# A macaron layer on one core: ScalarE rounds the steps' turns instead of VectorE, and the stages are ordered by new lengths

## The chip, the core and the metric

One core of a Trainium2 chip. The metric is the device time of one execution in microseconds, the median of several runs. TensorE is PE in the profile, VectorE DVE, ScalarE ACT, GpSimd POOL, SyncE SP (it only issues DMAs here); PEld is TensorE's loading of weights.

## What is computed

`x` has 4 batches of 512 rows of 512 numbers, all float32. Three sublayers, each added to `x`: half a mixture-of-experts FFN, an attention-like layer, half the FFN again.

```python
x = x + 0.5 * ffn(layernorm(x))
x = x + attn(layernorm(x))
x = x + 0.5 * ffn(layernorm(x))

def ffn(x):                                  # 8 experts, 2 per row
    gates = softmax over the two largest of x @ gate_w
    routed = sum over the two: gate * (gelu(x @ w1[e] + b1[e]) @ w2[e] + b2[e])
    return routed + gelu(x @ shared_w1 + shared_b1) @ shared_w2 + shared_b2

def attn(x):                                 # 32 heads x 8 channels x 8 frequencies
    z = causal_conv4(x @ W_mem); k_val, s_raw = z[..., :256], z[..., 256:]
    p_w = exp(clip(score_scale * s_raw, -20, 20) + log_w)
    phi = k_val[..., None] * theta
    num_re, num_im = cumsum(p_w * cos(phi)), cumsum(p_w * sin(phi))    # along the rows
    den = cumsum(p_w)
    out_re = sum over frequencies of (num_re * q_re + num_im * q_im) / den
    out_im = sum over frequencies of (num_im * q_re - num_re * q_im) / den
    y_val, y_gate = split(out_re @ W_re + out_im @ W_im)               # per head
    return (y_val * silu(y_gate)) @ W_out
```

## The kernel before

**The work.** The FFN runs as 8 jobs (`JOBS`: first FFN of batches 0 to 3, second FFN of batches 0 to 3). A job `q` loads rows (`fetch`), normalises them (`load`, `norm`), turns them (`turn`, 4 tiles of 128 rows), makes gate logits (`chunks`, `logits`, `rank`, `gates`, `gT`), and computes the shared expert (`hidden`, 4 matmul groups, and `acc`, 4). The jobs form 6 groups `g` (the last two have two jobs each). For each group the rows are sorted by expert into blocks of 128 (`place`, `scatter`, `slots`, `rows`), 15 blocks in a group of one job and 23 in one of two, 106 in all. A block is a chain over engines: GpSimd gathers its rows (`bring`), TensorE turns them (`x`, L907), ScalarE copies them to SBUF (`x`, L1081), TensorE multiplies (`one`, L916), ScalarE copies (`one`, L1089), TensorE turns (`mid`, L924), ScalarE applies gelu (`mid`, L1098), TensorE multiplies (`two`, L932), ScalarE scales (`two`, L1111), GpSimd adds the rows to DRAM (`add`, L1744).

The attention of a batch `b` has a head, 16 steps and a tail. Head: `a_load` to `a_turn`, `a_mem` (TensorE L951, and the convolution on VectorE, L1451 and L1454), `a_p`, `a_fall`, `a_den` (VectorE on 32 partitions), `a_q`, `a_spread`. Tail, per half of the heads: `c_out` (TensorE, then VectorE L1565, then a transfer into `outT`), `o_gate` (L985, silu on ScalarE, the product `o_mul` on VectorE), and at the end `o_rows` (L994).

**A step** `(b, n)` treats one half of the heads and one frequency on a 128 x 512 tile. It is what VectorE does most:
- `c_turn` on VectorE (`phases`): L1507 multiplies `k_val` by `theta`, in turns, and writes it as integers, which rounds it; L1509 multiplies again and subtracts the integers, which leaves the fraction of a turn. Both write into `trig[:, n % 2]`, so they wait until the sums of step n-2 have read it.
- `c_turn` on ScalarE (`waves`): absolute value (L1183), sine (L1185), cosine as a sine (L1186). The sine needs a table that gelu, silu and exp don't share; where the table changes a load stands in front.
- `c_scan` on VectorE: two running sums (L1520).
- `c_times`: two products with the queries `qx` (L1527, L1532), which SP loads per step (`c_query`).
- `c_sum`: two to four additions (L1543, L1545, L1551, L1553).

```python
VE.tensor_scalar(trig_int[:, s, 0, :], kept(b, half), th, None, ALU.mult).then_inc(*phase_int.of((b, n)))
vec.wait_ge(*phase_int.at((b, n)))
VE.scalar_tensor_tensor(trig[:, s, 1, :], kept(b, half), th, trig_int[:, s, 0, :],
                        ALU.mult, ALU.subtract).then_inc(*phase_made.of((b, n)))
```

**What sets the order.** Each engine is a queue in program order, and waits on semaphores at its head. The order of all stages is made when the program is built: `piece(engine, stage, length, *after)` names a stage's length in us and what it follows, `orders()` plays the queues with these lengths (an engine takes, of the stages that could start, the one with the longest way to the end), and each engine's loop issues its stages in that order. `HOP` is added to every handoff. Ways are corrected by tables of numbers, `PARTS`, `KINDS` and `URGENT`. The steps' stages on VectorE come behind everything else (`way[k] -= 10000.0`).

## Time and profile before

| | us |
|---|---|
| median of 3 runs | 1149.53 |
| lowest, highest | 1144.08, 1149.84 |
| the profiled execution | 1146.77 |
| its span | 1145.5 |
| TensorE busy | 1014.8 |
| VectorE busy | 728.5 |
| ScalarE busy | 642.0 |
| GpSimd busy | 486.2 |
| DMA, mean rate | 151 GB/s |

The span is the time from the first to the last instruction; the execution's own time is 1.3 us longer. A busy engine is one with an instruction under way. The page has the sums; where an engine waits, and for what, is in the views of waits, stretches and timelines.

### The profile page before, as it was taken

The page shows a single profiled execution, that of the slowest core. Times are in us where ns is not written, and L with a number is a line of the kernel's source. Part 1 is how long each engine was busy: PE and PEld are TensorE (multiplying, and loading weights), DVE is VectorE, ACT ScalarE, POOL GpSimd, SP SyncE. Part 2 cuts the span into 40 slices and gives each one's busy share as a digit, 9 for nine tenths or more (in the row PEclk, how much of TensorE's full clock was granted, in tenths as well). Part 3 has the DMA queues.
Part 4 walks back from the last instruction along what each step waited for, and adds up shares of the span by engine and source line. Part 5 has one row for each costly group of instructions (what it writes and reads, how often), then busy time and mean ns, then how long its engine had stood idle before and what let it go on. Part 6 is the DMA issues. An engine that isn't in the chain of part 4 may idle for free. (4 is left out here: it accounts for less than half of the span.)

```text
span 1145.5 us, 11321 instructions
## 1 busy us (share of the span) xinstructions
PE 1014.8 (89%) x3424; PEld 559.0 (49%) x3424; DVE 728.5 (64%) x1210; ACT 642.0 (56%) x1100; POOL 486.2 (42%) x449
## 2 busy tenths in 40 slices
PE   5989999779899898899999799978997999999992
PEld 3456544446345554344554445444554544446671
DVE  2310119879799988979998999899999721200000
ACT  4334334775674776655687666339778733224441
POOL 3444540556414334335334324714654412245642
PEclk9989999899999899999999899989999999999997
DMA  9966563793834776825587953347885735226666
GB/s 317 328 184 132 97 166 82 192 275 62 207 101 92 172 205 164 223 66 141 126 218 163 228 156 84 94 124 177 177 212 134 167 46 96 70 92 112 129 100 111
DMA packets 69201, 172.53 MB, mean 151 GB/s; under 512 B 12579, under 2 KB 12579, under 8 KB 67015
## 3 DMA queue, kind: packets, MB, share of 16 engines
q0 software_dynamic: 32576, 72.44, 34.8%
q1 hardware_dynamic: 35270, 89.74, 25.0%
q10 hardware_dynamic: 1296, 9.63, 2.4%
q8 instruction: 30, 0.49, 0.2%
q14 instruction: 29, 0.23, 0.1%
HBM read 112.86 MB, written 68.33 MB: 158 GB/s over the span
## 5 line engine op out<-in xcount | busy, mean ns | idle before, releaser
L932 PE MATMUL yps<-w_all,hidden_sb 128*128 x424 | 212.5, 626 | 15.7 <-ACT hidden_sb L1098 15.5
L916 PE MATMUL hps<-w_all,hidden_sb 128*128 x848 | 206.9, 389 | 11.0 <-ACT hidden_sb L1081 10.7
L1720 POOL DMA_INDIRECT xs<-x_normal,rows_i x106 | 121.8, 1149 | 198.9 <-PE xps L907 141.6
L916 PEld LDWEIGHTS hps<-w_all,hidden_sb 128*128 128x128 f32 x848 | 159.7, 195 | 49.4 <-issue 31.1
L1744 POOL DMA_INDIRECT x_rows<-ys,rows_i x56 | 105.2, 1878 | 147.6 <-ACT ys L1111 137.9
L1520 DVE TENSOR_TENSOR_SCAN run<-pwx,trig 128x512 f32<-128x512 f32 x128 | 149.4, 1209 | 20.8 <-ACT trig L1186 20.4
L1111 ACT ACTIVATE ys<-yps,slots 128x512 f32<-128x512 f32 x106 | 72.6, 686 | 110.8 <-PE yps L932 80.4
L932 PEld LDWEIGHTS yps<-w_all,hidden_sb 128*128 128x128 f32 x424 | 80.8, 200 | 87.9 <-issue 85.5
L874 PE MATMUL yps<-sw_sb,hidden_sb 128*128 128x512 f32 x256 | 120.1, 613 | 0.0
L862 PE MATMUL hps<-xnT,sw_sb 128*128 128x512 f32 x256 | 117.8, 612 | 2.1 <-issue 2.1
L1706 POOL DMA_INDIRECT slots<-told,dest_i x64 | 78.1, 1220 | 51.0 <-DVE cmp_a L1389 32.2
L994 PE MATMUL misc<-turns_sb,tail_sb 128*128 128x512 f32 x192 | 85.0, 592 | 0.0
L907 PE MATMUL xps<-ident,xs 128*128 128x128 f32 x424 | 66.8, 283 | 19.0 <-DMA xs<-x_normal,rows_i 6.4
L1527 DVE TENSOR_TENSOR trig<-run,qx 128x1024 f32<-128x1024 f32 x64 | 78.1, 1220 | 4.4 <-DMA qx<-q_cols 3.9
L862 PEld LDWEIGHTS hps<-xnT,sw_sb 128*128 128x128 f32 x256 | 48.9, 196 | 64.0 <-issue 63.5
L1532 DVE TENSOR_TENSOR qx<-run,qx 128x1024 f32<-128x1024 f32 x64 | 78.1, 1220 | 0.0
L1089 ACT COPY hidden_sb<-hps 128x256 f32<-128x256 f32 x106 | 39.4, 372 | 65.6 <-PE hps L916 60.6
L1744 POOL DMA_INDIRECT sum_rows<-ys,into_i x28 | 49.8, 1780 | 59.6 <-ACT ys L1111 56.9
L1081 ACT COPY hidden_sb<-xps 128x512 f32<-128x512 f32 x106 | 62.3, 590 | 21.3 <-PE xps L907 16.2
L874 PEld LDWEIGHTS yps<-sw_sb,hidden_sb 128*128 128x128 f32 x256 | 46.6, 192 | 54.8 <-issue 54.8
L907 PEld LDWEIGHTS xps<-ident,xs 128*128 128x128 f32 x424 | 52.2, 146 | 43.2 <-issue 24.6
L1183 ACT ACTIVATE trig<-trig 128x512 f32<-128x512 f32 x64 | 40.5, 632 | 54.8 <-DVE trig L1509 53.8
(201 smaller groups left out, 1541.8 us busy)
## 6 DMA issues: line engine op xcount, KB each, us to landing
qx<-q_cols SPq DMA_DIRECT2D x64, 512.0 KB
w_all<-in_w_experts SPq DMA_DIRECT2D x8, 1024.0 KB
x_normal<-xin SPq DMA_DIRECT2D x32, 256.0 KB
xin<-x_rows SPq DMA_DIRECT2D x32, 256.0 KB, 7.1
turns_sb<-in_w_out ACTq DMA_DIRECT2D x3, 1536.0 KB, 7.9
xin<-in_x SPq DMA_DIRECT2D x16, 256.0 KB, 6.0
sum_rows<-ys SPq DMA_DIRECT2D x16, 256.0 KB
xin<-sum_rows POOLq DMA_DIRECT2D x16, 256.0 KB, 5.9
```

The source lines that it names most:

```text
L862: t = PE.matmul(hps[:, bank, :], sw1_sb[:, c, n * P:(n + 1) * P], xnT[:, c, :], start=c == 0, stop=c == KC - 1)
L874: t = PE.matmul(yps[:, bank, :], hT[:, n, tb * P:(tb + 1) * P], sw2_sb[:, n, :], start=False, stop=n == SC - 1)
L907: t = PE.transpose(xps[:, bank, c * P:(c + 1) * P], xs[:, j % NX, c * P:(c + 1) * P], ident[:, :])
L916: t = PE.matmul(hps[:, bank, 0:H], xT[:, j % 2, c, :], w_all[:, bass.ds(expert[j] + c * H, H)], start=c == 0, stop=c == KC - 1)
L932: t = PE.matmul(yps[:, bank, :], hb[:, j % 2, ec, :], w_all[:, bass.ds(expert[j] + (KC * H + ec * D), D)], start=ec == 0, stop=ec == EC - 1)
L994: t = PE.matmul(misc[:, bank, :], yT[:, v, tb * P:(tb + 1) * P], wout_sb[:, v, :], start=v == 0, stop=v == VT - 1)
L1520: t = VE.tensor_tensor_scan(run[:, c, :], pwx[:, n // M, :], trig[:, n % 2, c, :], 0.0, ALU.mult, ALU.add)
L1527: VE.tensor_tensor(trig[:, n % 2, :, :], run[:, :, :], qx[:, n % NQX, :, :], ALU.mult).then_inc(*real_made.of((b, n)))
L1532: VE.tensor_tensor(qx[:, n % NQX, :, :], back, qx[:, n % NQX, :, :], ALU.mult).then_inc(*imag_made.of((b, n)))
L1706: GE.indirect_dma_start(slots_dram[g], bass.IndirectOffsetOnAxis(dest_i[:, g % 2, t, r:r + 1], 0), told[:, g % 2, first_tile + t, r, :], N ...
L1720: GE.indirect_dma_start(xs[:, j % NX, :], None, xn_rows[PAIR_OF[g]], bass.IndirectOffsetOnAxis(rows_i[:, g % 2, j:j + 1], 0)).then_inc(*xs ...
L1744: GE.indirect_dma_start(INTO[g][side], bass.IndirectOffsetOnAxis(at[:, g % 2, j:j + 1], 0), ys[:, j % 2, :], None, compute_op=ALU.add).the ...
```

## The change

ScalarE gets a stage `c_count` for each step: it multiplies `k_val` by `theta` and writes integers. VectorE's `c_turn` keeps only the multiplication and subtraction, and waits for ScalarE's count. ScalarE's wait for the sums of step n-2 stands in the new stage.

```diff
+            def count_turns(b, n):
+                half, m = divmod(n, M)
+                if b > 0 or n >= 2:
+                    last = (b, n - 2) if n >= 2 else (b - 1, STEPS + n - 2)
+                    act.wait_ge(*(out_summed if last[1] % M else added).at((*last, 0)))
+                if (b, n) == (0, 0):
+                    act.wait_ge(*weighing.at(21))
+                act.wait_ge(*convolved.at((b, half, CW - 1)))
+                SE.activation(trig_int[:, n % 2, 0, :], kept(b, half), ACT.Copy,
+                              scale=theta_sb[:, half, m:m + 1]).then_inc(*turns_counted.of((b, n)))
+
...
+                elif stage == "c_count":
+                    count_turns(*at)
...
             def phases(b, n):
                 half, m = divmod(n, M)
                 s = n % 2
-                th = theta_sb[:, half, m:m + 1]
-                if b > 0 or n >= 2:
-                    last = (b, n - 2) if n >= 2 else (b - 1, STEPS + n - 2)
-                    vec.wait_ge(*(out_summed if last[1] % M else added).at((*last, 0)))
-                vec.wait_ge(*convolved.at((b, half, CW - 1)))
-                VE.tensor_scalar(trig_int[:, s, 0, :], kept(b, half), th, None, ALU.mult).then_inc(*phase_int.of((b, n)))
-                vec.wait_ge(*phase_int.at((b, n)))
-                VE.scalar_tensor_tensor(trig[:, s, 1, :], kept(b, half), th, trig_int[:, s, 0, :],
+                vec.wait_ge(*turns_counted.at((b, n)))
+                VE.scalar_tensor_tensor(trig[:, s, 1, :], kept(b, half), theta_sb[:, half, m:m + 1], trig_int[:, s, 0, :],
                                         ALU.mult, ALU.subtract).then_inc(*phase_made.of((b, n)))
 
             def scan(b, n):
```

In the planner's steps, and the new `HOP`:

```diff
         def plan_step(i):
             b, n = STEPS_OF[i]
             half, m = divmod(n, M)
             free = [("DVE", ("c_sum", *STEPS_OF[i - 2]))] if i >= 2 else []
             piece("SP", ("c_query", b, n), 0.7, *[("SP", ("a_q", b, half * QH + g), 2.5) for g in range(QH)], *free)
-            piece("DVE", ("c_turn", b, n), 1.25, ("DVE", ("a_mem", b, half)), *free, *([] if i else [("DVE", ("w_soft", 1))]))
-            piece("ACT", ("c_turn", b, n), 2.0, ("DVE", ("c_turn", b, n)), table="sin")
-            piece("DVE", ("c_scan", b, n), 2.38, ("ACT", ("c_turn", b, n)), ("ACT", ("a_spread", b, half)),
+            piece("ACT", ("c_count", b, n), 0.5, ("DVE", ("a_mem", b, half)), *free, *([] if i else [("DVE", ("w_soft", 1))]))
+            piece("DVE", ("c_turn", b, n), 0.7, ("ACT", ("c_count", b, n)))
+            piece("ACT", ("c_turn", b, n), 1.81, ("DVE", ("c_turn", b, n)), table="sin")
+            piece("DVE", ("c_scan", b, n), 2.25, ("ACT", ("c_turn", b, n)), ("ACT", ("a_spread", b, half)),
                   *([("DVE", ("c_times", *STEPS_OF[i - 1]))] if i else []))
-            piece("DVE", ("c_times", b, n), 2.4, ("DVE", ("c_scan", b, n)), ("SP", ("c_query", b, n), 4.5))
-            piece("DVE", ("c_sum", b, n), 2.55 if m else 1.3, ("DVE", ("c_times", b, n)),
+            piece("DVE", ("c_times", b, n), 2.27, ("DVE", ("c_scan", b, n)), ("SP", ("c_query", b, n), 4.5))
+            piece("DVE", ("c_sum", b, n), 2.41 if m else 1.2, ("DVE", ("c_times", b, n)),
                   *([] if m or not b else [("PE", ("o_gate", b - 1, half * VH + VH - 1))]))
 
         def plan_tail(b):
...
-        HOP = 0.1
+        HOP = 0.2
```

Nearly every other length is new as well, and the three tables have new numbers:

```diff
                 s = ("x", g, j)
-                piece("PE", s, 0.6 if j % AT_ONCE else 1.3, ("POOL", ("bring", g, j), 3.8),
+                piece("PE", s, 0.45 if j % AT_ONCE else 0.95, ("POOL", ("bring", g, j), 3.8),
                       bank=[("xps", ("ACT", s))])
-                piece("ACT", s, 0.6, ("PE", s), ("PE", ("one", g, j - 2) if j >= 2 else ("acc", z, TB - 1)))
+                piece("ACT", s, 0.48, ("PE", s), ("PE", ("one", g, j - 2) if j >= 2 else ("acc", z, TB - 1)))
                 s = ("one", g, j)
-                piece("PE", s, 1.86, ("ACT", ("x", g, j)),
+                piece("PE", s, 1.74, ("ACT", ("x", g, j)),
...
                 s = ("mid", g, j)
-                piece("PE", s, 0.4, ("ACT", ("one", g, j)))
-                piece("ACT", s, 0.8, ("PE", s), *([("PE", ("two", g, j - 2))] if j >= 2 else []), table="gelu")
+                piece("PE", s, 0.23, ("ACT", ("one", g, j)))
...
-                piece("PE", s, 1.86, ("ACT", ("mid", g, j)), bank=[("yps", ("ACT", s))])
-                piece("ACT", s, 0.7, ("PE", s),
+                piece("PE", s, 1.73, ("ACT", ("mid", g, j)), bank=[("yps", ("ACT", s))])
...
-        PARTS = {"job": {2: 652, 3: -380, 4: -82, 6: -504},
...
+        PARTS = {"job": {1: 95, 4: -225, 6: -421},
...
```

What that does to the order, at three places. In these lists a line number is that of the file it is from, so L1526 of the change is L1520 of before. First VectorE, in batch 1 at step 1 (`c_scan`, `c_turn` of the next step, `c_times`, `c_sum`), before:

```order
L1520 SCALAR_TENSOR_TENSOR run<-pwx,trig 128x512 x2
L1507 TENSOR_SCALAR trig<-kval,small_sb 128x512
L1509 SCALAR_TENSOR_TENSOR trig<-kval,small_sb,trig 128x512
L1527 TENSOR_TENSOR trig<-run,qx 128x1024
L1532 TENSOR_TENSOR qx<-run,qx 128x1024
L1543 TENSOR_TENSOR trig<-trig 128x512
L1545 TENSOR_TENSOR qx<-qx 128x512
L1551 TENSOR_TENSOR outT<-outT,trig 128x512
L1553 TENSOR_TENSOR outT<-outT,qx 128x512
```

and now:

```order
L1526 SCALAR_TENSOR_TENSOR run<-pwx,trig 128x512 x2
L1515 SCALAR_TENSOR_TENSOR trig<-kval,small_sb,trig 128x512
L1533 TENSOR_TENSOR trig<-run,qx 128x1024
L1538 TENSOR_TENSOR qx<-run,qx 128x1024
L1549 TENSOR_TENSOR trig<-trig 128x512
L1551 TENSOR_TENSOR qx<-qx 128x512
L1557 TENSOR_TENSOR outT<-outT,trig 128x512
L1559 TENSOR_TENSOR outT<-outT,qx 128x512
```

L1507, the integer product, is gone; the rest stands as it did.

Second, ScalarE in batch 3 at step 3, now: L1186 is the new count, L1080, L1088 and L1097 are a block's `x`, `one` and `mid`, L1193 to L1196 the absolute value and the sines of the step.

```order
L1186 ACTIVATE trig<-kval,small_sb 128x512
L1080 COPY hidden_sb<-xps 128x512
L1088 COPY hidden_sb<-hps 128x256
L1097 ACT_TABLE_LOAD
L1097 ACTIVATE hidden_sb<-hps,bias_of 128x128 x2
L1193 ACTIVATE trig<-trig 128x512
L1195 ACT_TABLE_LOAD
L1195 ACTIVATE trig<-trig 128x512
L1196 ACTIVATE trig<-trig,half_pi 128x512
```

Between a count and its absolute value stand a block's copies and a gelu with its table load; before, there was no count, and the copies stood between one step's sines and the next.

Third, TensorE at block 13 of group 3. Before (L994 `o_rows`, L932 `two`, L916 `one`, L827 `turn`, L924 `mid`; a row that is left out repeats the one above it):

```order
L994 MATMUL misc<-turns_sb,tail_sb 128x512 x6
L932 ISA
L932 MATMUL yps<-w_all,hidden_sb 128x512
...
L916 ISA
L916 MATMUL hps<-w_all,hidden_sb 128x256
...
L827 MATMUL xps<-ident,xin 128x128 x4
L924 MATMUL hps<-ident,hidden_sb 128x128 x2
```

and now (L915 `one`, L931 `two`, L923 `mid`, L993 `o_rows`):

```order
L915 ISA
L915 MATMUL hps<-w_all,hidden_sb 128x256
...
L931 ISA
L931 MATMUL yps<-w_all,hidden_sb 128x512
...
L923 MATMUL hps<-ident,hidden_sb 128x128 x2
L993 MATMUL misc<-turns_sb,tail_sb 128x512 x6
```

Between `one` and the `mid` of the same block stood one `turn`; now a `two` does.

## Rows read from the trace of the kernel before

**Rows 1.** The page, engines: busy us, share of the span, instructions.

```profile
PE 1014.8 (89%) x3424; PEld 559.0 (49%) x3424; DVE 728.5 (64%) x1210; ACT 642.0 (56%) x1100; POOL 486.2 (42%) x449
```

**Rows 2.** Three stretches: from:to, length, busy us of each engine, granted clock, DMA share, GB/s.

```profile
0.00:173.00 173.00, 151.24 (x552) 86.95 (x553) 32.50 (x144) 67.57 (x130) 80.60 (x118) 0.98 0.72 203
173.00:910.00 737.00, 658.33 (x2140) 353.55 (x2140) 674.83 (x980) 491.95 (x797) 313.01 (x248) 0.96 0.64 156
910.00:1146.00 236.00, 205.22 (x734) 118.51 (x732) 21.13 (x87) 82.53 (x173) 92.60 (x84) 0.97 0.52 96
```

**Rows 3.** VectorE's waits in 173 to 910: us in total, times, longest us.

```profile
DVE run L1520 <- ACT trig L1186: 20.4, 11, 5.4
...
DVE stats_attn L1436 <- DMA xin<-sum_rows: 2.6, 3, 1.6
```

**Rows 4.** The chain of waits, by time: start us, us, what.

```profile
908.72 1.42 DVE tail_sb L1565 x2
...
979.85 0.99 PE xps L837 x8
...
984.47 0.79 PE xps L845 x8
...
1042.44 0.44 PE xps L907 x4
1042.88 1.73 PE hps L916 x8
1044.61 1.72 PE yps L932 x4
1046.32 0.22 PE hps L924 x2
```

**Rows 5.** TensorE's waits in 173 to 910.

```profile
PE hps L924 <- ACT hidden_sb L1089: 21.0, 9, 5.1
PE yps L932 <- ACT hidden_sb L1098: 13.3, 13, 1.9
...
PE hps L916 <- ACT hidden_sb L1081: 8.5, 3, 4.1
```

**Rows 6.** Groups of instructions, whole span: busy us, mean ns, idle before.

```profile
L1507 DVE TENSOR_SCALAR trig<-kval,small_sb 128x512 int32<-128x512 f32 x64 | 30.1, 470 | 0.1
...
L1186 ACT ACTIVATE trig<-trig,half_pi 128x512 f32<-128x512 f32 x64 | 45.3, 707 | 0.0
L1183 ACT ACTIVATE trig<-trig 128x512 f32<-128x512 f32 x64 | 40.5, 632 | 54.8 <-DVE trig L1509 53.8 <-issue 0.8
L1134 ACT ACTIVATE xin<-xin,rstd_ffn 128x512 f32<-128x512 f32 x32 | 23.4, 804 | 15.9 <-POOL rstd_ffn L1695 15.9
L1185 ACT ACT_TABLE_LOAD x39 | 50.0, 1283 | 0.7
```

**Rows 7.** VectorE's timeline, step 2 of batch 0: start us, us, instruction.

```profile
212.60 2.34 DVE L1520 TENSOR_TENSOR_SCAN run<-pwx,trig 128x512 f32<-128x512 f32 x2
214.85 0.47 DVE L1507 TENSOR_SCALAR trig<-kval,small_sb 128x512 int32<-128x512 f32 x1
215.35 0.75 DVE L1509 SCALAR_TENSOR_TENSOR trig<-kval,small_sb,trig 128x512 f32<-128x512 f32 x1
...
220.10 0.68 DVE L1553 TENSOR_TENSOR outT<-outT,qx 128x512 f32<-128x512 f32 x1
```

**Rows 8.** Timeline of ScalarE and TensorE at 639 to 642 us.

```profile
639.04 0.63 ACT L1183 ACTIVATE trig<-trig 128x512 f32<-128x512 f32 x1 [5.36 <-DVE trig L1509]
...
641.42 0.36 ACT L1089 COPY hidden_sb<-hps 128x256 f32<-128x256 f32 x1
...
641.84 0.69 PE L924 MATMUL hps<-ident,hidden_sb 128*128 128x128 f32 x2 [5.13 <-ACT hidden_sb L1089]
```

**Rows 9.** TensorE's longest wait in 0 to 173.

```profile
PE xps L827 <- POOL before L1782: 12.0, 1, 12.0
```

**Rows 10.** A stretch at the start, columns as in rows 2.

```profile
52.00:56.00 4.00, 4.00 (x15) 2.09 (x15) 1.13 (x9) 2.01 (x4) 0.88 (x1) 1.00 0.34 123
```

More of the change, by code:

```diff
@@ L335, in plan_job @@
[L335 to L337 removed]
+            piece("PE", ("chunks", q), 1.0, *kept_rows, *start[:1], bank=[("xps", ("ACT", ("chunks", q)))])
+            piece("ACT", ("chunks", q), 0.48, ("PE", ("chunks", q)), *([("PE", ("logits", q - 1))] if q else []))
@@ L431, in plan_head @@
                 free += [("DVE", ("a_den", b - 1))] if i == HALVES and b else []
-                piece("PE", s, 3.7, *kept_rows, weights, *free, *before, bank=[("misc", ("DVE", s))])
+                piece("PE", s, 3.45, *kept_rows, weights, *free, *before, bank=[("misc", ("DVE", s))])
                 piece("DVE", s, 3.0, ("PE", s))
@@ L502, in macaron @@
             ("steps", "c_count c_query c_turn c_scan c_times c_sum")) for name in names.split()}
-        PARTS = {"job": {2: 652, 3: -380, 4: -82, 6: -504},
-                 "blocks": {1: -389, 3: 798},
-                 "head": {},
-                 "tail": {0: -319, 1: 1414, 2: -298, 3: 283},
-                 "steps": {2: 407}}
-        KINDS = {("ACT", "mid"): -175,
-                 ("ACT", "norm"): 880,
-                 ("ACT", "o_rows"): 556,
-                 ("ACT", "one"): -59,
-                 ("ACT", "x"): -132,
-                 ("DVE", "a_stats"): -427,
-                 ("DVE", "c_out"): 632,
-                 ("DVE", "c_scan"): -201,
-                 ("PE", "a_mem"): 33,
-                 ("PE", "a_q"): -1,
-                 ("PE", "a_spread"): 1126,
-                 ("PE", "acc"): -144,
-                 ("PE", "gT"): -2768,
-                 ("PE", "hidden"): -415,
-                 ("PE", "logits"): 308,
-                 ("PE", "mid"): 197,
-                 ("PE", "o_gate"): 223,
-                 ("PE", "one"): 7,
-                 ("PE", "x"): 165}
@@ L527, in macaron @@
-        URGENT = {
-            ("ACT", "c_turn"): {0: -804, 1: 297},
-            ("ACT", "o_gate"): {0: 575},
-            ("ACT", "one"): {2: 853},
-            ("ACT", "turn"): {2: -1051, 6: 1015},
-            ("ACT", "two"): {2: -35, 4: -95},
-            ("ACT", "x"): {2: 309, 3: 158},
-            ("DVE", "a_mem"): {1: 15},
-            ("DVE", "c_out"): {2: -177},
-            ("DVE", "c_scan"): {0: 310},
-            ("DVE", "c_sum"): {0: 440},
-            ("DVE", "c_turn"): {0: -25, 1: 1196, 2: -92, 3: -968},
-            ("PE", "a_mem"): {3: -36},
-            ("PE", "a_q"): {1: -767},
-            ("PE", "c_out"): {0: 407},
-            ("PE", "mid"): {0: -81, 3: 26},
-            ("PE", "o_gate"): {0: 141, 2: 90},
-            ("PE", "o_rows"): {2: -237},
-            ("PE", "one"): {1: -297, 4: 117},
-            ("PE", "turn"): {6: 367},
-            ("PE", "two"): {3: 198, 4: 519, 5: 238},
-            ("PE", "x"): {2: -171, 4: -445},
+        PARTS = {"job": {1: 95, 4: -225, 6: -421},
+                 "blocks": {1: 159, 2: -387, 3: -112, 4: -234},
+                 "head": {0: 401, 3: -139},
+                 "tail": {1: -62},
+                 "steps": {0: -113, 1: 381, 3: 253}}
@@ new lines, in macaron @@
+        KINDS = {("ACT", "a_norm"): -296,
+                 ("ACT", "a_q"): 99,
+                 ("ACT", "c_turn"): 215,
+                 ("ACT", "one"): 104,
+                 ("ACT", "x"): 259,
+                 ("DVE", "a_den"): 39,
+                 ("DVE", "c_sum"): 397,
+                 ("DVE", "c_turn"): 268,
+                 ("DVE", "o_mul"): -464,
+                 ("PE", "a_mem"): 698,
+                 ("PE", "a_spread"): 338,
+                 ("PE", "acc"): -236,
+                 ("PE", "c_out"): -221,
+                 ("PE", "hidden"): -1445,
+                 ("PE", "o_gate"): -170,
+                 ("PE", "one"): -850,
+                 ("PE", "turn"): -472,
+                 ("PE", "two"): -1215,
+                 ("PE", "x"): -127,
+                 ("POOL", "bring"): 144,
+                 ("POOL", "load"): 410}
@@ new lines, in macaron @@
+        URGENT = {
+            ("ACT", "a_norm"): {0: -23},
+            ("ACT", "a_q"): {2: -484},
+            ("ACT", "a_turn"): {2: 144},
+            ("ACT", "mid"): {1: -26, 3: -206},
+            ("ACT", "norm"): {2: 405, 3: -574, 4: -133},
+            ("ACT", "o_gate"): {1: 294},
+            ("ACT", "one"): {1: -283},
+            ("ACT", "turn"): {6: 255},
+            ("ACT", "two"): {4: 548},
+            ("DVE", "a_mem"): {2: 207},
+            ("DVE", "c_turn"): {1: -532},
+            ("DVE", "place"): {0: -150, 3: 126},
+            ("PE", "a_q"): {1: 411},
+            ("PE", "a_spread"): {0: -548},
+            ("PE", "o_gate"): {1: -182, 2: -229},
+            ("PE", "two"): {5: 763},
+            ("PE", "x"): {2: -747},
```

76 lines of the change are left out of this document (38 added, 38 removed).

## The prediction

> **What bounds the kernel now.** I read the page's sums first, then cut the span at the two places where the load changes, then read waits and timelines inside the cuts.
>
> The sums [rows 1] show TensorE busy 1014.8 us of 1145.5, VectorE 728.5, ScalarE 642.0. That looks like a kernel bound by TensorE, and as an average over stages it misleads. The three stretches [rows 2] are different. Until 173 us and after 910 us VectorE has little to do (32.5 us of 173, 21.1 of 236) and TensorE is nearly full. Between them VectorE is busy 674.8 of 737 us (92%) and TensorE 658.3 (89%). 173 is where the first `a_mem` result reaches VectorE, 910 where its last `c_out` ends. In this middle stretch VectorE's own waits add up to 52 us, the first eight kinds of which are 47.8 [rows 3]; the largest, 20.4 us at 11 places, is a scan that waits for ScalarE's sines. So the middle is set by VectorE's list of work, and what follows 910 us is TensorE's remaining list. The chain of waits agrees from its far end: it begins on VectorE's last `c_out` at 908.7, goes over the transfer to `outT`, and then runs on TensorE through the last blocks [rows 4].
>
> TensorE's waits in the middle are 78.7 us (737 less 658.3), 42.8 of them for ScalarE on behalf of the expert blocks [rows 5]: 21.0 + 13.3 + 8.5. They cost nothing by themselves as long as VectorE is the later one.
>
> **The change, part by part.**
>
> *Removed from VectorE.* Each of the 64 steps had L1507 ahead of L1509. Its mean is 470 ns [rows 6], but what the queue gives back is the distance from its start to the next start: 214.85 to 215.35 [rows 7], 0.50 us. 64 x 0.50 = 32 us. All 64 lie in the middle stretch, where nothing else covers them. **-32.**
>
> *Added to ScalarE.* 64 copies with a per-partition scale, SBUF to SBUF, written as integers. No ACTIVATE of before writes integers, so the price is bounded: from below by `Abs` without pointers, 632 ns, from above by L1134 with scale and bias as pointers, 804; L1186 with one pointer takes 707 [rows 6]. I take 0.70, since one pointer is what the copy has: 45 us in all, on an engine with 492 of 737 us busy [rows 2]. It then has 537 of some 707, 76%. A copy calls for no table: the change's ScalarE program has 124 table loads, that of before 125. ScalarE is not the bound.
>
> The ScalarE page of the Trainium skill ("ScalarE: Activation LUTs", section Rules for kernel authors) says of `mul` and such: use VectorE, not ScalarE. The rows agree on the price (0.47 against some 0.70), and by the rule the sum would get worse by 45 - 30 = 15 us if both engines' work lay on one path. Nothing below rests on this: it is the loaded engine that is relieved.
>
> *The new handoff.* VectorE's L1509 used to follow its own integer product. Now the chain of a step is: sum of step n-2 on VectorE, count on ScalarE, L1509 on VectorE, sines on ScalarE, scan on VectorE. In the order of the change VectorE mostly has one pair of scans (212.60 to 214.85, 2.3 us [rows 7]) between the sum of n-2 and L1509 of n. The count needs 0.7 of that, so ScalarE must come to it within 1.6 us. The sines have 4.7 us of products and sums as cover and need 2.0 us, or 3.3 with a table load [rows 6]: a similar slack of 1.4 to 2.7, and 11 of 64 waited, 20.4 us in all [rows 3]. The bounds for the new handoff are therefore 0 and another 20; a late ScalarE delays both handoffs of a step only once, so I take the half. **+10.**
>
> *Drawn anew.* Against the trace the planner's old lengths were long: a block on TensorE 0.6 + 1.86 + 0.4 + 1.86 = 4.72 against 0.44 + 1.73 + 0.22 + 1.72 = 4.11 [rows 4]; a VectorE step 1.25 + 2.38 + 2.4 + 2.55 = 8.58 against 8.1 (212.60 to 220.10, and 0.6 for the last sum [rows 7]). The new ones are 4.15 and 7.63, with 0.2 per handoff. I counted TensorE's work (lengths from the chain) between the stages of a block in the middle stretch. Of before, 15 of 64 `mid` stages come less than 1 us of work after their `one`; of the change 3 of 62. `two` follows `mid` by less than 1.8 us of work in 12 of 62 and then in none of 61. The copy between `one` and `mid` takes 0.36 us alone, but behind sines it is late: for the `mid` at 641.84 TensorE had one `turn` as cover, ScalarE stood 5.36 us before the sines ahead of that copy, and TensorE waited 5.13 [rows 8]. So ScalarE's head-of-queue waits reach TensorE, and in the other direction a late TensorE holds ScalarE and with it the sines. With longer covers I expect most of the 42.8 us of TensorE's waits to go, and part of VectorE's 20.4; between nothing and 30 us of VectorE's 52 I take **-8**, the smaller part, as most of those waits are for transfers and handoffs whose place in the order is alike.
>
> *Ends of the stretch.* VectorE starts the middle when `a_mem(0, 2)` is done. Ahead of it TensorE now has two `x`, two `one` and a `mid` more of group 1: 0.88 + 3.46 + 0.22 = **+4.6**. After the last `c_out` transfer, from `o_gate(3, 3)` on, it has a `mid`, a `two`, `chunks` and `logits` more and two `x` fewer: 0.22 + 1.72 + 0.99 + 0.79 - 0.88 = **+2.8** [rows 4]. Outside the stretch TensorE is idle 21.8 us in front, 12.0 of it for the start [rows 9], which stays, and 30.8 behind [rows 2], the larger part of it after its last instruction. The rest is in small pieces; of it I take **-3** (bounds 0 and -8).
>
> Sum: 1146.8 - 32 + 10 - 8 + 4.6 + 2.8 - 3 = 1121.2 for the profiled execution. That one lies 2.8 below the median of the three runs (1149.5; they span 1144.1 to 1149.8), so I say **1122** for the median.
>
> *Does TensorE keep up?* The stretch would be 737 - 30 = 707. TensorE's busy time there is 658.3, less the 7.4 moved out of it: 651. It may wait 56 us where it waited 78.7. That needs 23 of the 42.8 us to go. Its granted clock of 0.96 there [rows 2] may rise a little with fewer gaps; I count nothing for it.
>
> *Queues moved past.* SP now issues the last expert's weights after the load of `slots(0)`. The DMA engines were busy only 0.34 of 52 to 56 us [rows 10], ahead of the first `one`, so 1 MB finds room there. I price it at nothing; its cover is the wait for the first gathered rows, and without that each us late is a us on the end. GpSimd's scatter of group 1 moves between the gathers of group 0: in two parts of four, each behind a gather, where TensorE has 16 us of other blocks' work; nothing.
>
> **The rivals.**
>
> *Order worth more (0.17).* VectorE's waits fall by 30, not 8. For it: the old lengths were 6 to 15% off and the covers grow nearly everywhere. Against: 32 of the 52 us are not for the sines. Time: 1122 - 22 = 1100; with the new handoff free, 1090.
>
> *TensorE becomes the bound (0.12).* Its waits stay at 78.7 because each is for a late ScalarE, which gets 45 us more work. The stretch is 651 + 79 = 730, 7 shorter; with +4.6 and +2.8 the time is 1147: no change. It decides once more than 56 us of waits remain; half-way gives 1136.
>
> *The count holds VectorE (0.07), slower.* ScalarE takes its queue in order, and ahead of most counts stand copies that wait for TensorE. If the count is late as the sines were where they waited (1.85 us each) at every second step, that is 32 x 1.85 = 59 us, and the late L1509 delays sines and scans behind it: 1122 - 10 + 59 = 1171. It decides from (10 + 27.5) / 64 = 0.59 us of wait per step on, where the time is that of before. Against it: in the order of the change three entries on average stand between a count and its sines, as many as VectorE's scans and L1509 cover. This is the mechanism by which the rule of the ScalarE page, cited above, would hold here.
>
> *The copy doesn't relieve VectorE (0.02).* The 64 rows of L1507 are gone from its program, so only a much slower write of integers could undo this.
>
> **How the numbers follow.** Forecast 0.62: its bounds are 1122 - 18 (handoff free, starts better) and 1122 + 14 (handoff 20, no gain from the order), 1104 to 1136. Below lie 0.17, above 0.21. A range of **1096 to 1144** leaves out about 0.06 below and 0.12 above. About 0.5%, 5.7 us, is what a measurement of this kernel tells from no change, so faster means below 1143.8: the forecast, the first rival, and a third of the second, 0.84. Within 0.5%: the rest of the second and of small cases, 0.09. Slower: 0.07.
>
> **What would show it.** VectorE's busy sum near 698 and ScalarE's near 687; the new copy at 0.70 us; VectorE's last `c_out` at some 880 instead of 910, and TensorE's end some 218 us later; TensorE's waits for `mid` under 10 us; VectorE's L1509 waiting for the count some 10 us in sum. Wrong if L1509's waits exceed 30 us, if the copy takes over 1 us, or if TensorE is busy over 95% of the middle and VectorE waits for banks and `a_mem`.

## The result, and the profile after

The change is slower. Four runs gave 1174.5 us in the median (1166.2 to 1178.0) beside 1148.4 of before; the ratio is 1.022, interval 1.017 to 1.028. The forecast was 1122, its range ended at 1144. The profiled execution took 1178.0, its span is 1176.7.

The sums of the profile page after, and its row of TensorE's granted clock in 40 slices:

```profile
PE 1024.8 (87%) x3424; PEld 568.4 (48%) x3424; DVE 699.7 (59%) x1146; ACT 678.8 (58%) x1163; POOL 522.8 (44%) x449
...
PEclk9979999989989999988999999998999999999997
```

VectorE is down from 728.5 to 699.7 and ScalarE up from 642.0 to 678.8, as the edit wants it [rows 1]. GpSimd (POOL) went from 486.2 to 522.8, although its 449 instructions are the same: nothing in the prediction has that.

The three stretches after, cut where the first `a_mem` result reaches VectorE and behind the last `c_out` (columns as in [rows 2]):

```profile
0.00:190.00 190.00, 160.91 (x573) 94.12 (x574) 30.66 (x142) 70.15 (x136) 82.87 (x120) 0.95 0.68 193
190.00:935.00 745.00, 653.03 (x2104) 352.78 (x2103) 648.33 (x919) 520.65 (x846) 344.04 (x244) 0.95 0.62 150
935.00:1177.00 242.00, 210.91 (x750) 121.55 (x748) 20.70 (x86) 87.96 (x182) 95.93 (x85) 0.96 0.54 99
```

The front takes 190 us where it took 173, the middle 745 where it took 737 with 26.5 us more work on VectorE, the end 242 where it took 236. TensorE's waits in the middle are 745 - 653 = 92 us; they were 78.7.

VectorE's longest waits in the middle (of the first row 23.6 us is the wait that ends at 189.6 and belongs to the front), and the new copy on ScalarE with who waits for it:

```profile
DVE low_rows L1463 <- PE misc L950: 26.8, 4, 23.6
DVE run L1526 <- ACT trig L1196: 21.3, 18, 5.2
DVE trig L1515 <- ACT trig L1186: 19.3, 15, 3.3
DVE rows_i L1433 <- DMA slots<-slots: 11.8, 2, 6.8
DVE tail_sb L1583 <- ACT tail_sb L1206: 11.5, 6, 5.1
```

```profile
L1186 ACT ACTIVATE trig<-kval,small_sb x64: 704/722/766, 199.9 to 919.0; 128x512 int32<-128x512 f32 x64
its engine sat idle before it (us, times) until:
  DVE outT L1557: 10.6, 5
```

The copy takes 0.72 us, the sines' wait is where it was (21.3, before 20.4), and the new handoff costs VectorE 19.3 us. The list explains at most why 32 us shrank to some 13. It doesn't explain a loss.

The chain of waits says more. An issue is the time that GpSimd spends on starting one indirect transfer, that is, one whose row numbers stand in a tile. After, among the chain's 35 longest pieces (start, length, what), stand these:

```profile
396.96 6.43 POOL xs L1726
...
490.25 10.13 POOL sum_rows L1750
...
608.10 5.20 POOL sum_rows L1750
```

A gather's issue usually takes 1.0 us, an addition's 1.6. These pieces are 5 to 10 long, and the program's end hangs on them. The chain of before can't be set beside it: its view goes back to 908.6 us only. Two runs of the next sections, whose chains reach back to the start, have no piece on GpSimd over 2.03 us: the one with the same order and the count on VectorE, and the one with a pause in each step.

### The profile page after: what moved, and what is told of

Its sections match the earlier page's. It is cut to its first block, busy times and chain, and to the rows that moved or that the text cites. A ratio compares the mean times of both kernels' runs of the same rounds, so it can differ in the third digit from the quotient of the medians.

```text
span 1176.7 us, 11356 instructions
## 1 busy us (share of the span) xinstructions
PE 1024.8 (87%) x3424; PEld 568.4 (48%) x3424; DVE 699.7 (59%) x1146; ACT 678.8 (58%) x1163; POOL 522.8 (44%) x449
## 4 chain that ended last, share of the span: by engine, by line
PE 50%; DMA 11%; ACT 11%; issue 11%; POOL 10%; DVE 6%; another core or an unknown queue 0%; SPq 0%; POOLq 0%; ACTq 0%; DVEq 0%
PE hps L915 10%; PE yps L931 8%; PE misc L993 7%; PE yps L873 5%; PE hps L861 5%; PE misc L959 4%; DMA x_rows<-ys,rows_i 4%; PE misc L950 3%; DMA xs<-x_normal,rows_i 3%; PE xps L906 2%; POOL xs L1726 2%; POOL slots L1712 2%; ACT L1097 2%; POOL sum_rows L1750 2%; DMA xin<-sum_rows 1%
## 5 line engine op out<-in xcount | busy, mean ns | idle before, releaser
L1726 POOL DMA_INDIRECT xs<-x_normal,rows_i x106 | 134.4, 1268 | 245.9 <-PE xps L906 207.8
L915 PE MATMUL hps<-w_all,hidden_sb 128*128 x848 | 218.9, 404 | 24.1 <-ACT hidden_sb L1097 23.0
L931 PE MATMUL yps<-w_all,hidden_sb 128*128 x424 | 203.1, 605 | 5.3 <-ACT hidden_sb L1097 3.1
L915 PEld LDWEIGHTS hps<-w_all,hidden_sb 128*128 128x128 f32 x848 | 165.2, 203 | 62.0 <-issue 41.4
L1526 DVE TENSOR_TENSOR_SCAN run<-pwx,trig 128x512 f32<-128x512 f32 x128 | 149.4, 1208 | 21.5 <-ACT trig L1196 21.3
L1750 POOL DMA_INDIRECT x_rows<-ys,rows_i x56 | 98.8, 1764 | 111.9 <-ACT ys L1110 105.9
L931 PEld LDWEIGHTS yps<-w_all,hidden_sb 128*128 128x128 f32 x424 | 79.3, 194 | 69.5 <-issue 65.8
L1712 POOL DMA_INDIRECT slots<-told,dest_i x64 | 88.0, 1375 | 50.5 <-DVE cmp_a L1401 26.9
L1080 ACT COPY hidden_sb<-xps 128x512 f32<-128x512 f32 x106 | 61.7, 582 | 82.8 <-PE hps L915 56.4
L993 PE MATMUL misc<-turns_sb,tail_sb 128*128 128x512 f32 x192 | 90.2, 622 | 1.6 <-DVE tail_sb L1587 1.6
L1750 POOL DMA_INDIRECT sum_rows<-ys,into_i x28 | 64.5, 2303 | 48.7 <-ACT ys L1110 45.0
L1097 ACT ACTIVATE hidden_sb<-hps,bias_of 128x128 f32<-128x128 f32 x212 | 66.0, 366 | 6.7 <-PE hps L923 5.3
L923 PE MATMUL hps<-ident,hidden_sb 128*128 128x128 f32 x212 | 43.2, 288 | 29.9 <-ACT hidden_sb L1088 25.7
```

The lines of the kernel that those rows point to most:

```text
L915: t = PE.matmul(hps[:, bank, 0:H], xT[:, j % 2, c, :], w_all[:, bass.ds(expert[j] + c * H, H)], start=c == 0, stop=c == KC - 1)
L931: t = PE.matmul(yps[:, bank, :], hb[:, j % 2, ec, :], w_all[:, bass.ds(expert[j] + (KC * H + ec * D), D)], start=ec == 0, stop=ec == EC - 1)
L993: t = PE.matmul(misc[:, bank, :], yT[:, v, tb * P:(tb + 1) * P], wout_sb[:, v, :], start=v == 0, stop=v == VT - 1)
L1097: t = SE.activation(hb[:, j % 2, ec, :], hps[:, bank, H + ec * P:H + (ec + 1) * P], ACT.Gelu, bias=bias_of[:, g % 2, ec, j:j + 1])
L1526: t = VE.tensor_tensor_scan(run[:, c, :], pwx[:, n // M, :], trig[:, n % 2, c, :], 0.0, ALU.mult, ALU.add)
L1712: GE.indirect_dma_start(slots_dram[g], bass.IndirectOffsetOnAxis(dest_i[:, g % 2, t, r:r + 1], 0), told[:, g % 2, first_tile + t, r, :], N ...
```

## Experiments: two orders, and who counts

**Old order, ScalarE counts.** Before with the change's `count_turns` on ScalarE, and every engine's order kept. `AHEAD` names, for each step, the stage that its count is put ahead of:

```diff
         ORDERS = orders()
+        AHEAD = [
...
+        for at, stage in zip(STEPS_OF, AHEAD):
+            ORDERS["ACT"].insert(ORDERS["ACT"].index(stage), ("c_count", *at))
```

> The order of before on every engine, kept stage for stage; only the count of whole turns goes from VectorE to ScalarE, each of the 64 put in ScalarE's list ahead of the first stage that in the trace of before started after the sum of step n-2 had ended (or right ahead of its own sines, where there was none). Theory A (the new order lost the time, the handoff is cheap): 1148 - 32 + 10 = 1126, and with waits at a third of the steps 1135. Theory B (the handoff itself holds VectorE, whatever the order): 1148 or more.

Measured 1176.5 (ratio 1.024). But one count stood badly: that of step (3, 0) waited 28.1 us for batch 3's kept memory at the head of ScalarE's queue.

**New order, VectorE counts.** The change with `c_count` dropped from ScalarE's list and both products in `phases` as before:

```diff
         ORDERS = orders()
+        ORDERS["ACT"] = [s for s in ORDERS["ACT"] if s[0] != "c_count"]
```

> The order of the change on every engine, stage for stage, with the count back on VectorE ahead of its own product (ScalarE's 64 counts are dropped). Theory A: VectorE gets its 32 us back on the path and loses some 10 of handoff, so 1174 + 20 = 1194 or more, far above before: the order alone is bad by over 40 us. Theory B: the handoff was what cost, so it falls to between 1150 and 1170, the new order by itself costing only what its head shows (some 19 us).

Measured **1140.7** (0.993, interval 0.989 to 0.997). Both theories miss. The new order is by itself 8 us faster than before, and moving the count costs 34 us on top of it. That is more than the whole new handoff wait.

**No count at all**, in either order, and **a count that nobody reads**:

```diff
-                VE.scalar_tensor_tensor(trig[:, s, 1, :], kept(b, half), th, trig_int[:, s, 0, :],
+                VE.scalar_tensor_tensor(trig[:, s, 1, :], kept(b, half), th, kept(b, half),
```

The sines have a scale of 0.01 in these three. In the third, ScalarE still counts.

> The order of the change with no count at all: neither VectorE nor ScalarE makes the whole turns, and VectorE's product subtracts the kept memory itself (the sines get a small scale, so their values are not the reference's). It stands beside the run with the same order and the count on VectorE (1141). Theory V (the middle is set by VectorE's list): 1141 - 32 = 1109. Theory T (the middle is set by TensorE and ScalarE in turn, VectorE follows): 1130 to 1141, so that taking the work away gives a third at most.

> The same in the order of before, beside before's 1148. Theory V: 1148 - 32 = 1116. Theory T: 1138 to 1148.

> The change as it is, ScalarE making its 64 counts at their places and with their waits, but VectorE's product doesn't read them and doesn't wait for them (it subtracts the kept memory, and waits for the sum of step n-2 as before did; values not the reference's). Less the run without any count it gives the price of ScalarE's 46 us of load and of its waits at the head of its queue; the change's 1174.5 less it gives the price of the handoff. Theory L (load and head-of-queue waits on ScalarE): 1160 or more. Theory H (handoff, VectorE late for the count): within 10 us of the run without counts, so some 1115 to 1125.

Measured 1170.7, 1158.7 and 1171.3. This settles three things. Taking 32 us off VectorE and giving them to nobody makes the new order 30 us **slower** (1140.7 to 1170.7). ScalarE's 46 us of load add nothing there (1170.7 to 1171.3). The handoff adds 3 at most (1171.3 to 1174.5, within the spread of the executions). What costs in the new order is that VectorE's instruction is gone. In the old order the same step costs 10 us (1148.4 to 1158.7, executions from 1148.7 to 1167.2).

**Old order, the one count put better:**

> The first experiment again (old order, the count on ScalarE), with one count placed better: in the first run the count of step (3, 0) stood ahead of a_q(3, 0) and held ScalarE 28.1 us and TensorE 19.6 us, since I had put it by the sum of step n-2 alone and not by the kept memory of batch 3. It now stands ahead of a_q(3, 2). Theory A (order, not handoff): 1176 - 28 = 1148, down to 1140 if the late statistics of the last jobs come forward too. Theory B: the stall was hidden by other work, 1165 or more.

Measured 1166.8: the badly placed count was worth 10 us, and the old order loses by the move too (18 us). Here 8 of the 18 lie between no count (1158.7) and ScalarE's count; how they divide between its load and the handoff no run shows.

## Experiments: the pause

Where GpSimd's issues are long, the timeline of the change shows VectorE without a pause. GpSimd and VectorE, from 741.6 us on (start, length, engine, line, operation, operands, idle time before):

```profile
741.64 0.68 DVE L1559 TENSOR_TENSOR outT<-outT,qx 128x512 f32<-128x512 f32 x1
742.35 0.68 DVE L1362 CAST bias_parts<-xps 27x512 fp32r<-27x512 f32 x1
742.86 8.57 POOL L1712 DMA_INDIRECT slots<-told,dest_i  x1 [0.30 <-issue]
742.96 2.32 DVE L1526 TENSOR_TENSOR_SCAN run<-pwx,trig 128x512 f32<-128x512 f32 x2
745.20 0.71 DVE L1515 SCALAR_TENSOR_TENSOR trig<-kval,small_sb,trig 128x512 f32<-128x512 f32 x1
745.85 1.21 DVE L1533 TENSOR_TENSOR trig<-run,qx 128x1024 f32<-128x1024 f32 x1
746.98 1.21 DVE L1538 TENSOR_TENSOR qx<-run,qx 128x1024 f32<-128x1024 f32 x1
748.12 0.67 DVE L1549 TENSOR_TENSOR trig<-trig 128x512 f32<-128x512 f32 x1
...
749.92 0.67 DVE L1559 TENSOR_TENSOR outT<-outT,qx 128x512 f32<-128x512 f32 x1
751.74 0.96 POOL L1712 DMA_INDIRECT slots<-told,dest_i  x1 [0.30 <-issue]
751.88 0.74 DVE L1463 TENSOR_SCALAR low_rows<-misc,small_sb 32x512 f32<-32x512 f32 x1 [1.28 <-PE misc L950]
```

Each VectorE instruction starts some 0.07 us before the one ahead ends, from 742.96 to 750.59. GpSimd's issue, usually 0.97 us, starts at 742.86 and ends at 751.43: 0.84 behind VectorE's first pause. Every VectorE instruction of that run has two operands in SBUF. The next issue, in the pause, takes 0.96.

In before a step had a pause of its own, because L1509 waits for the result of the instruction right ahead of it (the timeline of before, at its longest issue):

```profile
711.06 7.30 POOL L1706 DMA_INDIRECT slots<-told,dest_i  x1 [0.30 <-issue]
...
715.26 2.32 DVE L1520 TENSOR_TENSOR_SCAN run<-pwx,trig 128x512 f32<-128x512 f32 x2
717.51 0.45 DVE L1507 TENSOR_SCALAR trig<-kval,small_sb 128x512 int32<-128x512 f32 x1
718.00 0.75 DVE L1509 SCALAR_TENSOR_TENSOR trig<-kval,small_sb,trig 128x512 f32<-128x512 f32 x1
```

717.51 + 0.45 = 717.96, and L1509 starts at 718.00: a pause of 0.04 us. In most steps the other waits for VectorE's own results have an instruction in between, and make no pause. The change took L1507 away, and the pause with it.

It took away a second thing. The issue above ends at 718.36, 0.78 behind the end of the scans (717.58) but only 0.40 behind L1507's end. In the change an issue needed 0.84 from the pause to its end, so I take this one as let in at L1507's start. L1507 has one operand in SBUF. So L1507 offered GpSimd 0.45 us with one such operand and a pause behind it. I counted the 27 gathers and scatters over 5 us in all the traces. Each ends 0.75 to 0.87 us behind the end of a VectorE instruction. Behind that end stands a pause in 11 of them, without a pause an instruction with at most one SBUF operand in 7, and in 9 one with two. A one-operand instruction as long as L1507 and without a wait was not run.

Four runs put the pause to the test. In the first, one column is written in each step, with a wait for its end:

```diff
             def phases(b, n):
...
+                k = STEPS_OF.index((b, n))
+                VE.tensor_scalar(gap[:, k:k + 1], theta_sb[:, half, m:m + 1], 1.0, None, ALU.mult).then_inc(*gap_made.of((b, n)))
+                vec.wait_ge(*gap_made.at((b, n)))
                 VE.scalar_tensor_tensor(trig[:, s, 1, :], kept(b, half), theta_sb[:, half, m:m + 1], trig_int[:, s, 0, :],
```

The second has the instruction without the wait. The third is the run without any count, with instruction and wait. The fourth adds no instruction, only `vec.wait_ge(*scanned.at(last_scan[0]))` at that place.

> The change with one more instruction per step on VectorE: a TENSOR_SCALAR of one column (128 x 1) from one SBUF operand, right ahead of the product that reads the count, with a wait for its own end. Theory G: GpSimd's indirect transfers read their indices from SBUF and are held while VectorE runs instructions with two SBUF operands back to back (in the change the issues of 1 to 1.6 us last 7 to 11 us at four places and end where VectorE pauses); the old count, with one SBUF operand and a wait behind it, was the pause of each step. Then this run gets the 34 us back that the move cost, less some 64 x 0.1: 1140 to 1150. Any other theory (order, load of ScalarE, handoff): VectorE gets 6 us or more of work, 1174 to 1185.

> The same without the wait for its own end: one small one-operand instruction in VectorE's stream, no pause. If it is the operand form that lets GpSimd in: as g1, 1140 to 1150. If it is the pause: 1170 or more.

> The run without any count (new order, 1171) with the small instruction and its wait in each step. Theory G: now VectorE's 32 us of relief can show: 1141 - 32 + 6 = 1115, up to 1130. If it stays at 1165 or more, theory G is wrong.

> The change with a pause alone: VectorE's product waits for the end of the last scan ahead of it (in 33 of 64 steps the instruction right ahead), no instruction added. Theory G with the pause as the opening: 1145 to 1160, as half of the steps get one. If the opening needs an instruction with one SBUF operand: 1170 or more.

Measured **1144.6** (ratio 0.996, 0.992 to 0.999), 1172.2, 1139.1, 1158.7 (1.007). An instruction and a pause, 0.18 us per step together, give back 30 us. The same instruction without a pause gives nothing within the spread. Pauses alone, in half of the steps, give half (executions from 1149.7 to 1169.9), so a pause is enough without a one-operand instruction. The third run shows the pause's price again (1170.7 to 1139.1), but not the 1115 to 1130 that VectorE's relief should have brought. That part of the expectation fell.

The pause in the timeline of the first run (L1518 is the new instruction), and below it the missing one in the second. There a scatter's issue of 14.28 us ends at 310.19. It had passed over such an instruction at 301.71, and it ends 0.78 behind the last scan, where L1586, a product of the tail with one operand in SBUF and one in PSUM, follows without a pause:

```profile
309.81 0.69 DVE L1588 TENSOR_TENSOR tail_sb<-misc,tail_sb 128x512 f32<-128x512 f32 x1
310.42 0.14 DVE L1518 TENSOR_SCALAR gap<-small_sb 128x1 f32<-128x1 f32 x1
310.60 0.75 DVE L1520 SCALAR_TENSOR_TENSOR trig<-kval,small_sb,trig 128x512 f32<-128x512 f32 x1
```

```profile
295.91 14.28 POOL L1715 DMA_INDIRECT slots<-told,dest_i  x1 [0.30 <-issue]
...
301.71 0.12 DVE L1517 TENSOR_SCALAR gap<-small_sb 128x1 f32<-128x1 f32 x1
...
307.09 2.32 DVE L1529 TENSOR_TENSOR_SCAN run<-pwx,trig 128x512 f32<-128x512 f32 x2
309.34 0.68 DVE L1586 TENSOR_TENSOR tail_sb<-misc,tail_sb 128x512 f32<-128x512 f32 x1
309.94 0.14 DVE L1517 TENSOR_SCALAR gap<-small_sb 128x1 f32<-128x1 f32 x1
310.00 0.74 DVE L1518 SCALAR_TENSOR_TENSOR trig<-kval,small_sb,trig 128x512 f32<-128x512 f32 x1
```

The groups of GpSimd's gathers and scatters of before, of the change and of the run with the pause (busy us, mean ns):

```profile
L1720 POOL DMA_INDIRECT xs<-x_normal,rows_i x106 | 121.8, 1149 | 198.9 <-PE xps L907 141.6 <-DVE into_i L1430 36.7 <-issue 16.9
...
L1706 POOL DMA_INDIRECT slots<-told,dest_i x64 | 78.1, 1220 | 51.0 <-DVE cmp_a L1389 32.2 <-issue 18.1 <-DVE cmp_b L1401 0.7
```

```profile
L1726 POOL DMA_INDIRECT xs<-x_normal,rows_i x106 | 134.4, 1268 | 245.9 <-PE xps L906 207.8 <-DVE into_i L1442 17.5 <-issue 14.8
...
L1712 POOL DMA_INDIRECT slots<-told,dest_i x64 | 88.0, 1375 | 50.5 <-DVE cmp_a L1401 26.9 <-issue 17.7 <-DVE cmp_a L1420 2.6
```

```profile
L1731 POOL DMA_INDIRECT xs<-x_normal,rows_i x106 | 123.7, 1167 | 250.6 <-PE xps L908 209.6 <-DVE into_i L1444 21.2 <-issue 13.2
...
L1717 POOL DMA_INDIRECT slots<-told,dest_i x64 | 75.2, 1175 | 51.5 <-DVE cmp_a L1403 26.9 <-issue 17.3 <-DVE bias_of L1425 3.3
```

For this table I counted in each trace, from 190 us to the last `c_out`: the longest run of VectorE's instructions in which none starts over 0.015 us behind the end of the one ahead, and the sum of the lengths of GpSimd's 152 to 155 indirect issues.

| kernel | median us | longest run without a pause | GpSimd's issues | longest |
|---|---|---|---|---|
| before | 1148.4 | 11.1 | 248.8 | 7.3 |
| new order, VectorE counts | 1140.7 | 10.2 | 236.4 | 3.2 |
| the change | 1174.5 | 23.6 | 275.0 | 10.7 |
| old order, ScalarE counts, count replaced | 1166.8 | 22.3 | 279.3 | 21.1 |
| new order, no count | 1170.7 | 28.0 | 288.0 | 15.5 |
| old order, no count | 1158.7 | 28.8 | 278.3 | 21.1 |
| count unread | 1171.3 | 35.0 | 292.1 | 14.2 |
| change + instruction, no wait | 1172.2 | 27.7 | 270.0 | 14.3 |
| change + wait alone | 1158.7 | 11.2 | 249.4 | 6.5 |
| change + pause | 1144.6 | 10.2 | 235.8 | 3.2 |
| no count + pause | 1139.1 | 10.2 | 237.2 | 3.2 |

All kernels of the table without the pause have stretches over 20 us and take 1158 or more. All with one at least every 11.2 us take 1159 or less, and the change with one in every step takes 1144.6.

The medians are of all executions, the other columns of the profiled one alone, and the two don't always go together. The profiled one of "old order, no count" took 1148.7, the lowest of its four, with an issue of 21.1 us in it; that of "change + wait alone" took 1149.7. So a long issue doesn't always reach the end. That the pause is worth 30 us is shown, twice (1174.5 to 1144.6, 1170.7 to 1139.1); that it acts through GpSimd's issues is read from the traces. TensorE's waits for gathered rows in the middle are 16.4 us in the change and 6.7 with the pause. No run frees GpSimd in another way.

## Experiments: the head, and what bounds the middle

**The head.** Before with two things of the change's head, GpSimd's scatter of group 1 between gathers and the `place` that it needs:

```diff
+        behind("PE", ("place", 1), ("logits", 1))
+        behind("POOL", ("scatter", 1, 0), ("bring", 0, 4))
+        behind("POOL", ("scatter", 1, 1), ("bring", 0, 5))
```

> Before, with one thing of the change's head: place(1) on TensorE right behind logits(1), and GpSimd's scatter of group 1 in two parts behind the gathers (0,4) and (0,5), as in the change. By my prediction this costs nothing: 1148. By the theory that those 8 scatters (1.27 us each, 10 us) hold the gathers and additions that TensorE waits for, it costs 5 to 15: 1153 to 1163; they also leave 10 us of GpSimd's chain ahead of the first attention statistics, so it could come out some us faster (1140) if gathers were never late.

Measured 1159.9 (1.010, 1.006 to 1.015): 11.5 us, which I had priced at nothing. In its trace the first `a_mem` result comes at 176.3, 5.6 later than in before; the rest comes behind it.

**The head of before in front of the new order**, first as it is, then with the pause, then with the count on VectorE:

```diff
+        for engine, names in HEAD.items():
+            head = [(s.split(",")[0], *map(int, s.split(",")[1:])) for s in names.split()]
+            ORDERS[engine] = head + [s for s in ORDERS[engine] if s not in head]
```

> The change with the head of before: on each engine the stages that before has ahead of a_mem(0,2) come first and in before's order (so GpSimd's scatter of group 1 stands behind the additions of group 0 again, and four gathers fewer of group 1 are ahead), the rest in the order of the change. If the 19 us by which the change reaches a_mem(0,2) later are simply added to the end: 1174 - 19 = 1155, and the middle stays at some 745. If the middle takes them up (its waits are for work of the blocks, which the old head leaves later): 1170 or more.

> The change with the pause in each step (1144.6) and the head of before on every engine (GpSimd's scatter of group 1 behind the additions of group 0). The old head was worth 9 us without the pauses, and the scatter alone cost before 11.5: 1133 to 1138. If the middle takes the head's gain up: 1144.

> The order of the change behind the head of before, with the count on VectorE (1140.7 with the new head). If the head's loss is separate: 5 to 9 less, 1132 to 1136. If not: 1141.

Measured 1165.6, 1139.6 (0.994, 0.989 to 0.998) and 1142.0 (0.996, 0.993 to 0.998). The old head brings 9 us to the change, 5 with the pause, and nothing where VectorE counts (1140.7). In the traces the first `a_mem` result comes 10.5, 3.4 and 3.1 us sooner with it (179.1, 176.2, 175.9). The last two pairs lie within the spread, so whether the middle takes up what the head gains isn't shown.

**The pause in the old order, and a second pause per step** (ahead of the additions):

> The order of before with the count on ScalarE (1166.8 without pauses) and the pause in each step. If the pause is all that was lost: 1166.8 - 30 = 1137. If the old order hangs on VectorE more than the new one, so that its relief shows: 1148 - 32 + 12 + 10 = 1138 too, down to 1125; 1148 or more if ScalarE's load costs in this order.

> The change with two pauses per step, the second ahead of the four additions and subtractions. If GpSimd's issues still wait for VectorE on the path of TensorE (they are still 2 us and more at some ten places): 5 to 10 below 1144.6, so 1135 to 1140. If the one pause is enough: 1144 to 1150, 64 x 0.18 = 12 us of VectorE that may be hidden.

Measured 1149.5 and 1143.7. In the old order the pause gives back 17 of the 18 us that the move had cost, and ScalarE's count then neither gains nor loses against before (1.003, 1.000 to 1.006). A second pause changes nothing.

**What sets the middle.** From the run without a count but with the pause, 448 of 512 columns are left out of the two additions to `outT` in 56 steps (VectorE 52 us less than the run with the pause). From the run with the pause, half of the matmuls of `hidden` and `acc` in the jobs 2 to 5 are left out:

```diff
-                VE.tensor_tensor(re, re, trig[:, n % 2, 0, :], ALU.add).then_inc(*out_summed.of((b, n, 0)))
+                VE.tensor_tensor(re[:, 0:64], re[:, 0:64], trig[:, n % 2, 0, 0:64], ALU.add).then_inc(*out_summed.of((b, n, 0)))
...
+                terms = KC // 2 if 2 <= q <= 5 else KC
```

> The run without any count and with the pause in each step (1139), and the two running sums of 56 steps on 64 of the 512 columns (the output is then not the reference's), which takes 56 x 2 x some 0.5 = 56 us more from VectorE. If VectorE sets the middle: 1139 - 56 = 1083, at least below 1115. If TensorE with its waits for ScalarE and for gathers sets it: 1130 to 1140.

> The change with the pause in each step (1144.6), and in the jobs 2 to 5, which lie in the middle, the matmuls of hidden and of acc over 2 of their 4 chunks (the output is then not the reference's): 64 matmuls of 0.46 us each, 29 us less for TensorE, VectorE's and ScalarE's work as it was. If TensorE sets the middle: 1144.6 - 29 = 1115, up to 1122 with longer waits. If VectorE does, or the handoffs between all engines in their fixed order: 1135 to 1144.

Measured 1138.9 and 1151.4. The middle of the run with the pause, of the one with shorter sums, and of the one with fewer matmuls (columns as in [rows 2]):

```profile
180.00:895.00 715.00, 643.19 (x2098) 348.77 (x2097) 656.12 (x983) 519.83 (x845) 301.63 (x244) 0.96 0.65 156
```

```profile
183.00:893.00 710.00, 643.60 (x2091) 347.78 (x2090) 603.48 (x983) 480.91 (x780) 289.63 (x244) 0.95 0.66 157
```

```profile
187.00:908.00 721.00, 612.03 (x1968) 330.58 (x1967) 656.22 (x983) 520.05 (x845) 304.71 (x244) 0.93 0.65 155
```

VectorE's busy time fell by 52.6 us and the middle by 5. TensorE's fell by 31 and the middle grew by 6, at a granted clock of 0.93 instead of 0.96. The expectation took half too little away: the trace has two records for a matmul, 128 fewer in all (3424 to 3296), and at 0.45 us each that is 58 us. Some 27 of them came back, as the matmuls that were left took longer. Neither engine's list of work sets the middle by itself. Which chain of handoffs does is left open; no run here takes ScalarE's or the gathers' part away alone.

## Why the prediction was wrong

- **"The middle is set by VectorE's list of work": this step failed**, and the 32 us stood on it. VectorE was 92% busy and its waits were short, but TensorE beside it was 89% busy [rows 2], and I took the busier for the binding one. The chain that I read as agreeing [rows 4] begins at 908.6 because its view goes no further back; it says nothing of the middle. With the pauses kept, 21 us less of busy time (no count, 1139.1 against 1140.7) and 72 less (shorter sums, 1138.9) gave nothing. These runs are in the new order. In the old one, 20 us less for VectorE together with ScalarE's counts gave nothing either (1149.5).
- **What the removal did to others was missing.** I priced L1507 as work, and it was also the step's only regular pause, and an instruction with one SBUF operand. A pause put back is worth 30 us (1174.5 to 1144.6), the whole loss and more. No row that I chose could show it; the lengths of single GpSimd issues beside VectorE's timeline would have: before has one of 7.3 us.
- **The copy, 0.70:** 0.72. VectorE 699.7 where I said 698, ScalarE 678.8 where I said 687. The price is right, but ScalarE's busy time rose by 37 where 64 copies of 0.72 are 46.
- **The new handoff, +10:** VectorE waited 19.3 us, just inside the bounds of 0 and 20. Between the count unread and the change lie 3 us, within the spread.
- **Drawn anew, -8:** with the count left on VectorE the new order brings 7.7 against before in all, head and end included. The size is right by luck, the reason isn't: TensorE's waits for `mid` went from 21.0 to 25.3 in the middle, and 21.2 new ones for gelu stand ahead of `one`, where I had expected under 10.
- **Ends of the stretch, +4.6 and +2.8, and "Queues moved past", nothing:** the first `a_mem` result reached VectorE at 189.6, 18.9 later. In nine of the ten other profiles with this head it came at 178.6 to 182.4, 8 to 12 later than in before (170.7), in one at 186.6. The scatter between gathers is one miss: alone it made `a_mem` 5.6 later and the end 11.5. The end of the program, behind the last `c_out`, took 6 us more (242 for 236), where I had said nothing in sum (+2.8 - 3). The rest at the front in the profiled execution of the change begins with a stall at 77 us, where TensorE waited 4.07 and its granted clock was 0.77 from 75 to 90 us (1.00 in the run with the same order and VectorE counting); what started it is left open.
- **"TensorE may wait 56 us":** it waited 92. As a rival, "TensorE becomes the bound" fell with the run with fewer matmuls.
- **The rival "the count holds VectorE", 1171,** has the right time for a wrong reason: L1515 waited 0.30 us per step, under its 0.59, and without reading the count the time stayed at 1171.3. So the rule of the Trainium skill ("ScalarE: Activation LUTs", section Rules for kernel authors) that I cited isn't what the runs confirm: with it the sum would have got worse by 15 us through ScalarE's load, and in the new order that load cost 0.6.

## What to carry over

An instruction that is removed takes along the room that it left to others: before pricing it by its length, look at what other engines get done beside it and behind it. Where GpSimd issues indirect DMAs beside a full VectorE, compare the lengths of single issues (here 1 us, and up to 21 where VectorE didn't pause), and put a small instruction with a wait for its own end into the loop (0.18 us a step for 30 us). A busy share of 92% proves no bound, and neither does a chain whose view begins behind the stretch in question; shorten the engine's work in one run and see whether the end moves.

The best versions here, the new order with VectorE counting (0.993) and the change with the pause and the old head (0.994), are some 0.6% below before, little more than a measurement can tell.

## What the runs showed of the hardware

- GpSimd's indirect issues were held while VectorE ran instructions with two SBUF operands back to back, for up to 21.1 us. The Trainium skill ("SBUF — State Buffer", section Who interferes with whom) says that an instruction of VectorE with two SBUF inputs contends with a GpSimd instruction that reads SBUF; these issues read their row numbers from there, so the trace agrees.
- In the longest cases the boundaries between 7 to 24 back-to-back instructions let no waiting issue through. With a pause of 0.04 us a step (310.56 to 310.60) the change's longest issue in the middle is 3.2 us; in the old order one of 7.9 is left. An instruction with one SBUF operand let an issue in at its start, ahead of any pause (L1507, 0.45 us, and L1586, 0.68 us: the issues end 0.78 behind 717.58 and 309.41); one of a single column, 0.12 us, was passed over (301.71), and with it the time stayed at 1172.2. In other cases an issue got in at a boundary of two two-operand instructions; what decides it is open. Whether the reading of the row numbers or the writing of the descriptors is what is held was not tried.
- Taking matmuls away lowered TensorE's granted clock from 0.96 to 0.93 in the middle, and the matmuls that were left took longer (the mean of `acc` 654 ns for 605), so 58 us of matmuls taken away were 31 us less of busy time, and ended in no gain.
